# First attention of a four-layer kernel: another order for the logits, the table work and the head masks

## The reference, cut to what matters

```
q, k, v = x @ Wq + bq, x @ Wk + bk, x @ Wv + bv        # (b, 256, 16 heads, 8)
relpos  = clip(j - i, -63, 0) + 63                      # i query, j key
rk, rq  = e @ Wrk + brk, e @ Wrq + brq                  # e: table of 64 rows, normed
c2c = einsum('bqhd,bkhd->bhqk', q, k)
c2p = einsum('bnhd,whd->bhnw', q, rk)[:, :, i, relpos]
p2c = einsum('bnhd,whd->bhwn', k, rq)[:, :, relpos, i]
logits = where(causal, (c2c + c2p + p2c) / sqrt(24), -big)
out = softmax(logits) @ v @ Wo + bo
```

## Time and profile before

| | us |
|---|---|
| median of 3 runs (lowest, highest) | 3783.09 (3774.97, 3783.92) |
| span of the profiled execution (no other time is listed for it) | 3806.1 |
| the attention's steps in it, from the first L550 to the last L594 | about 71.8 to 554 |
| busy in the span: PE, PEld, DVE, ACT, POOL | 3386.1, 2274.3, 2409.4, 1861.9, 1726.8 |

### The profile page before, as it was taken

One profiled execution on the slowest core, in us unless ns is written; L12 is line 12 of the kernel. 1 busy time (PEld: TensorE's weight loads), 2 busy tenths in 40 slices (PEclk: granted clock), 3 DMA queues, 4 the chain that ended last, 5 costly groups with the idle time before them and its releaser, 6 DMA issues. The chain is left out here.

```text
span 3806.1 us, 70702 instructions
## 1 busy us (share of the span) xinstructions
PE 3386.1 (89%) x24704; PEld 2274.3 (60%) x24704; DVE 2409.4 (63%) x5387; ACT 1861.9 (49%) x5051; POOL 1726.8 (45%) x1887
## 2 busy tenths in 40 slices
PE   6888888869999989999997999988999999998496
PEld 3555553547777756666663444436777777776274
DVE  3888762546666656666663444457888888888134
ACT  4666664456666635444444000036666667664033
POOL 2555541327777743333330000013676676676644
PEclk8999998989999999999998999998999999999697
DMA  4888850030000000000002777752552222222423
GB/s 132 215 210 209 210 135 11 1 76 1 2 2 2 1 1 1 2 2 1 2 1 67 159 152 152 151 101 80 122 122 71 79 78 72 79 76 65 141 69 106
DMA packets 312553, 300.58 MB, mean 79 GB/s; under 512 B 72137, under 2 KB 227721, under 8 KB 311946
## 3 DMA queue, kind: packets, MB, share of 16 engines
q1 hardware_dynamic: 307594, 286.58, 30.7%
q0 software_dynamic: 4608, 9.48, 0.8%
HBM read 237.45 MB, written 58.53 MB: 78 GB/s over the span
## 5 line engine op out<-in xcount | busy, mean ns | idle before, releaser
L2413 DVE TENSOR_TENSOR_SCAN a_h<-a_dA,a_dBu_psum 128x512 f32<-128x512 f32 x512 | 596.0, 1205 | 119.0 <-issue 106.3
L2298 POOL TENSOR_TENSOR a_h<-a_h,main_g 128x512 f32<-128x512 f32 x256 | 384.2, 1503 | 256.6 <-DVE a_h L2413 246.5
L1246 POOL TENSOR_SCALAR a_probs<-a_probs,a_row_inv 128x128 f32<-128x128 f32 (+1 forms) x512 | 381.2, 765 | 163.9 <-DVE a_row_inv L1209 163.9
L1712 DVE SCALAR_TENSOR_TENSOR m_hidden<-m_h_psum,m_gate_spread 128x512 f32<-128x512 f32 x256 | 176.9, 692 | 263.6 <-PE m_h_psum L1650 251.1
L179 POOL TENSOR_TENSOR main_g<-main_g,main_s 128x512 f32<-128x512 f32 x28 | 44.0, 1606 | 649.8 <-ACT main_g L161 649.8
L1515 POOL TENSOR_TENSOR r_position_q<-r_turned_q 128x512 f32<-128x512 f32 x128 | 160.0, 1272 | 387.3 <-DVE r_turned_q L1560 387.3
L2009 PE MATMUL a_dBu_psum<-a_B_diag,a_dt_u_turned 64*128 64x128 f32 x4096 | 317.1, 289 | 20.6 <-DVE a_h L2413 19.8
L1472 ACT ACTIVATE r_probs<-r_logits_psum,r_neg_max 128x256 f32<-128x256 f32 x512 | 235.5, 476 | 141.0 <-DVE r_neg_max L1566 141.0
L2009 PEld LDWEIGHTS a_dBu_psum<-a_B_diag,a_dt_u_turned 64*128 64x128 f32 x4096 | 257.9, 188 | 74.9 <-issue 71.0
L1151 ACT ACTIVATE a_probs<-a_logits,a_neg_max 128x128 f32<-128x128 f32 (+1 forms) x512 | 226.7, 446 | 128.3 <-DVE a_neg_max L1195 128.3
L2032 PE MATMUL a_y_psum<-main_ident,a_h 128*128 128x128 f32 x2048 | 274.8, 276 | 7.8 <-POOL a_h L2298 6.7
(11 more groups left out here) (522 smaller groups left out, 7620.3 us busy)
## 6 DMA issues: line engine op xcount, KB each, us to landing
m_gate_spread<-m_gate_rows SPq DMA_DIRECT2D x64, 1024.0 KB, 8.2
main_g<-a_b_c_rows SPq DMA_DIRECT2D x256, 256.0 KB, 3.2
a_band_rows<-main_g SPq DMA_DIRECT2D x64, 512.0 KB, 3.0
a_B<-a_band_rows SPq DMA_DIRECT2D x192, 128.0 KB, 3.3
a_A<-a_band_rows SPq DMA_DIRECT2D x192, 128.0 KB, 3.4
f_x_expert<-f_x_rows SPq DMA_DIRECT2D x16, 322.5 KB
f_x_rows<-a_zero SPq DMA_DIRECT2D x16, 320.0 KB, 5.0
f_stage_w<-L_ffn_up_weights SPq DMA_DIRECT2D x9, 512.0 KB, 6.7
```

What stands on the lines that cost most here:

```text
L1246: ins = nc.gpsimd.tensor_scalar(pr[:, h % NPR, tile[t]], pr[:, h % NPR, tile[t]], rinv[:, p % NST, q:q + 1], None, ALU.mult)
L2298: tt(h[:, r, :, :], h[:, r, :, :], Cs[:, g % NCS, :, :], ALU.mult).then_inc(hc_pool, 1)
L2413: nc.vector.tensor_tensor_scan(flat, dA[:, M % NDA, q, k, :, :].rearrange("p n t -> p (n t)"), db[:, 2 * (g % 2) + k, :], 0.0, ALU.mult, A ...
```

## The change

Three orders are changed, and nothing else. On PE `logit` of the next step is issued at the end of a step, ahead of `bands`, where it stood at the head of its own step, behind them. On DVE all three table operations stand ahead of `keep_band`. On POOL the heads of sequence b + 1 are masked inside sequence b, between `mask_bands(b, 1)` and `mask_bands(b, 2)`, where those of b + 2 had been masked behind it. The waits are as before.

```
@@ block.tensor @@
+                logit(0)
                 for p in range(LAST + 1):
-                    if p < NQ:
-                        logit(p)
                     for what, b in first(p):
                         make(what, b)
                     for g in range(4):
...
                     if 2 <= p < NQ + 2:
                         weigh(p - 2)
+                    if p + 1 < NQ:
+                        logit(p + 1)
                     if band_of(p) is not None:
                         bands(band_of(p), p)
@@ block.vector @@
                     if p < NQ:
                         turn_table()
                         turn_table()
+                        turn_table()
                     if band_of(p) is not None:
                         keep_band(band_of(p))
-                    if p < NQ:
-                        turn_table()
@@ block.gpsimd @@
                 for b in range(NSEQ):
-                    for j in range(3):
-                        mask_bands(b, j)
+                    mask_bands(b, 0)
+                    mask_bands(b, 1)
+                    if 1 <= b < NSEQ - 1:
+                        mask_heads(b + 1)
+                    mask_bands(b, 2)
                     mask_bands(b, 3)
-                    if b + 2 < NSEQ:
-                        mask_heads(b + 2)
```

## The result

| | median us (lowest, highest) | ratio to before, 95% interval |
|---|---|---|
| before, beside the changed kernel | 3780.89 (3774.97, 3783.92) | 1 |
| changed | 3746.59 (3744.2, 3749.67) | 0.9915 [0.9903, 0.9927] |

34.3 us faster; 47 were forecast, with 3736 in a range of 3716 to 3764. The profiled spans are 3806.1 and 3742.4, but only part of their difference is the change's: from the first L550 to the last L594 the attention takes 448.4 (69.2 to 517.6), where it took 482.1. The rest is in stages that the change does not touch.

The account below looks back on a forecast made before the run. GpSimd's order, heads masked ahead of the next window, was taken to stop VectorE at boundaries. 3.0 + 0.15 + 0.19 + 0.15 = 3.5 per sequence, 45.5 for 13, about 2 more: 47, so 3736; range 3716 to 3764, own range 3725 to 3743.

Parts of the forecast that it names:

- the stop at the boundary: Between two sequences VectorE waits 3.32 before its first logits; blamed on GpSimd masking heads ahead of the next window's bands.
- Masks, 2.4 per boundary: Part of the 3.0 gained at each boundary of two sequences that was credited to masking the heads earlier.
- the 3.0 taken off: At a boundary VectorE was to start its first logits at 256.7 in place of 259.67.
- The slack: First window masked 12.7 to 13.5 after the last band's copy, VectorE wanting it at 14.3: 0.8 to 3.2 spare.
- The 3.9 of landing: Median time for a load to land, added to the end of A's issue to date the first window; 4.7 at most.
- The sum: 3.5 per sequence, 45.5 for 13, about 2 at the 14th boundary; together 47, rounded down.
- Rival 1: Data come late, so the stop at the masked window stays, shorter, ended by a DMA; 21 gained, 3762; chance 0.12.
- PE's new order, 0.6 per boundary: At each boundary, the part of the 3.0 gain credited to PE issuing the next step's logits ahead of the bands.
- 0.49 in the other steps: Per sequence away from the boundary: VectorE's 0.15 band wait gone in two steps, PE's 0.19 saved in step 4b + 1.
- Rival 2: Port meetings with GpSimd stretch VectorE's table operations, 17 at worst; 31 gained, 3752; chance 0.07.
- The heads cost nothing ahead of windows 2 and 3: GpSimd done with window 2 at + 26.1 after the copy, VectorE wanting it at + 28.5, despite 3.66 of heads ahead.
- rival 4: Slower: heads make windows 2 and 3 late, stopping VectorE and ScalarE mid-sequence; loss of 16, 3799; chance 0.04.

Follow-up runs that it names:

- masks_only: The kernel before with only the heads' masking moved inside the sequence, PE and VectorE orders unchanged; 3746.65 us, ratio 0.9918 to before.

## Why the prediction was right, and where it was not

- **What bounded the kernel.** Right: the stop at the boundary was GpSimd's order. Changing it alone gives 32.2 of the 34.3.
- **Masks, 2.4 per boundary.** Right in size: 14 of them are 33.6, measured 32.2. In masks_only VectorE starts 15.2 behind the copy where the window is early, for 17.7 before, which is 2.5.
- **"With the 3.0 taken off ... 14.3 are left. The slack is 0.8 to 3.2, so it holds, but narrowly."** This is the step that failed. Over 12 boundaries the window was ready 12.2 to 15.7 after the copy, 14.0 in the mean, not 12.7 to 13.5, and VectorE could start at 13.6 to 13.8, not 14.3: the slack was about nothing. At the boundary shown the window took 298.63 - 282.98 = 15.7, which is 3.0 more than behind the earlier trace rows: 0.9 because SyncE was still busy with the window before, 0.6 for the write of the band before, which by then stood ahead of this one, 0.45 in longer issues of the write and the weights, 0.4 in those of B, and 0.55 more waiting for the write. I took SyncE's chain from a row where it had idled ahead of the copy, and so forgot that with idle gone it starts late. The 3.9 of landing is there too, but by luck: the earlier trace rows counts it from the start of an issue, and I added it to the end of one; from its start this load took 4.5. The bounds held this ("if landings stretch beyond the slack, less"), the value taken did not.
- **The sum.** 47 less the 17.6 of mask stops that are left is 29.4, the profiled attention gained 33.7 and the runs 34.3; the 4 to 5 between are not accounted for. Rival 1, the data late, is what happened in a small form, with 17.6 of stops in place of its 28 (2 at each of 14). So 3746.59 lies in the stated range of 3716 to 3764, but outside the forecast's own 3725 to 3743.
- **PE's new order, 0.6 per boundary, and 0.49 in the other steps.** They brought nothing that can be told: changed and masks_only are at 0.9915 and 0.9918. PE's 0.63 ahead of L539 did go, as forecast. But VectorE, ready at 13.6 to 13.8 behind the copy in place of 15.2, meets a window that is done at 14.0, and in step 4b + 1 a wait that I hadn't priced doubled: PE's for the sums' reciprocal (L718, behind the copy of the band) is 18.2 for 8.6, in 98.4 to 460.
- **Ports.** Rival 2's sign came, L327 and L329 up by a tenth or more (625 to 700 ns), but not its 17 us: the stretch is 0.6 per sequence, and VectorE has it to spare. Its sum has a slip: 47 less 17 is 30, not 31.
- **The heads cost nothing ahead of windows 2 and 3.** Right: no wait of GpSimd's for PE, and rival 4 did not come. **DVE's waits for PE, "about 20".** Right, 18.5, though half of that is mask stops under a wrong name.
- **DMA share "near 0.94".** 0.88; the same 25.6 of transfer in a sequence of 28.44 would be 0.90.

## What to carry to other kernels

When a stop is removed, ask which queue feeds the next one, and price its chain with that queue busy, not as it ran when it had time to idle. Work taken off an engine that waits for data only makes the wait longer; take a cause away at the source (fewer or smaller loads) to see the pace behind it. Where a wait ends 0.12 to 0.13 behind the end of another engine's work time after time, as at the 14 boundaries of the kernel before, suspect that engine, whatever the view says, and test it by moving that work.

## What was not expected of the hardware

The issuing instruction of a load takes 0.607 to 0.617 us in the median on SyncE for 64 as for 128 KB, so that 32 of them fill 19.7 of a sequence of 28.4 while the share of busy time shows nothing of it. A write of 512 KB lands in 3.0 us in the median before, in 4.5 in the changed kernel, where loads stand close around it, and in 3.7 with half the bytes in these. And single table operations took 1.97 to 2.72 us in one profile, where most take 0.62.
